# Grouping the attention exponentials by three slices and splitting three products into float16 parts

## The chip, the cores and the metric

The kernel runs on one core of one Trainium2 chip. The metric is the device time of one execution, in microseconds. The program is a chain of two attention layers with a mixture-of-experts layer between them and a "wave" layer fused behind the second attention. Five engines work side by side and meet at semaphores: TensorE (PE, with its weight loads listed apart as PEld), VectorE (DVE), ScalarE (ACT), GpSimd (POOL) and SyncE (SP, here only the issuer of DMAs).

## The reference, cut to what matters

```python
x = x + xattn0(layernorm(x), ctx, mask)      # 16 heads of 16, 2048 queries, 1601 keys
x = x + ffn(layernorm(x))                    # 2 shared and 8 routed experts, top 2
x = x + xattn1(layernorm(x), ctx, mask)
x = x + sqrt((n @ cos(theta + theta_noise))**2 + (n @ sin(phi + phi_noise))**2)   # n = layernorm(x)

def xattn(query, key, ...):
    q = query @ wq + bq;  k = key @ wk + bk;  v = key @ wv + bv
    alpha = softmax(q k^T / 4 + mask)        # per head
    return (alpha @ v) @ wo + bo

scores = sigmoid(u @ centroids)              # the router of ffn, u = layernorm(x)
```

All of it is float32. x is 2048x256, ctx is 1601x256.

## The kernel before, in words

`attention(nc, g, layer)` is called twice. Its main loop goes over 16 units (`u`): four chunks `c` of 512 queries, times four quads `q` of four heads. Inside a unit it goes over 13 key tiles `t` of 128 keys (the last has 65). So each layer has 208 tiles, the two layers 416. A tile has four slices `j`, one per head, each a bank of 128 keys x 512 queries.

What each engine does for a tile:

- TensorE, `scores(G)` (line 1260): the scores of a slice are one float32r matmul with 52 contraction rows (16 rows of the head three times, because keys and queries are held as a high and a low part, and 4 rows for shift and mask). Heads alternate between the partitions from 0 and those from 64 of `kst` and `qst` (`a` is 0 or 1, `tile_position=(HALF * a, 0)`), so two slices, one in each half of the array's rows, can run side by side. Before the change a group `G` is such a pair, and a tile has two groups (`PAIRS = 2 * KT` in a unit).
- ScalarE (line 708): one exponential for each group, 128x1024, from two PSUM banks to the float32 tile `prob`. `prob` is a ring of three tiles (`P_RING`).
- TensorE, `outputs(u, t)` (line 1274): four float32 matmuls of `v` with the four slices, side by side in four column groups of 32. Each float32 matmul is listed as two matmuls, so a tile shows x8. They gather in one of the two banks `outp`.
- VectorE, `finish(u)` (lines 903 to 914): at the end of a unit it copies the sums, takes reciprocals and scales.

The eight PSUM banks are six for scores and two for `outp`. The six are a ring of `S_RING = 3` groups of two banks. `scores(G)` waits for `exp_done >= G - S_RING + 1`, the exponential that frees its banks. The order on TensorE is written out: three groups ahead of the loop, then for each tile two `scores` (three groups ahead of the tile's own) and one `outputs`.

Between the tiles TensorE does side work at fixed tiles `t`, one piece after `outputs`: `project_out` (line 1299, quad 0 of chunks 1 to 3, t = 5, 6, 8, 9), `turn_tokens` (transposes, line 1306; quad 1 at t = 3, 4 for the next chunk's queries, quad 2 at t = 3, 5 for the finished chunk), `query` (line 1313, quad 1, t = 6, 7, 9, 10: one 128x512 float32 matmul each), in layer 0 `logits` (line 1322, quad 2, t = 8), in layer 1 `wave` (line 1330, quad 2 at t = 7, 8, 10, 11 and quad 3 at t = 4, 5, 8, 9). Side work uses the idle one of the `outp` banks. VectorE empties it: `untangle` (line 936), `split_query` (943, 945), `take_turned` (987 to 997), `take_logits` (1001), `take_wave` (1010 to 1014). In layer 0 VectorE also cuts the expert weights into float16 halves (924, 926).

Before the loop each layer projects keys (line 1142), turns the first chunk (1109), projects its queries (1149), bounds the scores, and projects values (1216). After the loop the last chunk's side work runs with nothing beside it. The sine of the wave angles is taken by ScalarE at the start of layer 1 (line 653). A branch for unsafe scores (`safe_is_off`) is not taken.

Of the kernel before, what the change touches and what calls it, by code (L numbers as in the profile page):

```python
# [4 lines left out]
F32 = mybir.dt.float32  # L5
# [8 lines left out]
P = 128  # L14
# [16 lines left out]
PARTS = 2  # L31
HALF = P // 2
# [30 lines left out]
PAIRS = 2 * KT  # L63
S_RING = 3
# [6 lines left out]
class Core:  # L71
    pass

# [23 lines left out]
def attention(nc, g, layer):  # L97
# [3 lines left out]
    with ExitStack() as es:  # L101
# [10 lines left out]
        xnT = sb("xnT", [P, DH, CH], F32)  # L112
        qparts = sb("qparts", [P, DH, PARTS, CH], F32R)
        amat = sb("amat", [P, DH, P], F32R)
        wq = sb("wq", [P, DH, D], F32)
# [18 lines left out]
        if first:  # L134
            gains = sb("gains", [P, 2, DH], F32)
            more = sb("more", [P, 2 * CH], F32)
# [9 lines left out]
        bqrow = flat_prob[0:1, KT * D + 7 * D:KT * D + 9 * D].rearrange("p (b n) -> p b n", b=2)  # L146
        slow_kst = flat_prob[:, 0:KV + 1]
# [25 lines left out]
        outp = [banks[:, 2 * S_RING + i, :] for i in range(2)]  # L173
        turn = [score[0][:, 0, :], score[0][:, 1, :]]
        pj = [score[1][:, 0, :], score[1][:, 1, :], score[2][:, 0, :]]
        nrm = score[2][:, 1, :]
        slow_score = [banks[:, 4 * i:4 * i + 4, :].rearrange("p b s -> p (b s)") for i in range(2)]
        tailbank = [score[0][:, 0, :], score[0][:, 1, :], score[1][:, 0, :], score[1][:, 1, :]]
# [25 lines left out]
        on_ready, evac_step = sem("on_ready"), sem("evac_step")  # L204
        if first:
            rows_step, rows_ready, rows_stored, xhl_stored = (
                sem(n) for n in ("rows_step", "rows_ready", "rows_stored", "xhl_stored"))
            gain_loaded, gain_ready, high_done, piece_done = (
                sem(n) for n in ("gain_loaded", "gain_ready", "high_done", "piece_done"))
# [3 lines left out]
        else:  # L213
            gathered = [sem(f"gathered{c}") for c in range(NC)]
            added, wave_done, power_ready, rooted, final_done, out_stored = (
                sem(n) for n in ("added", "wave_done", "power_ready", "rooted", "final_done", "out_stored"))
# [67 lines left out]
        def _(sp):  # L284
# [10 lines left out]
            def load_queries(u):  # L295
                b, c, quad = u % Q_RING, u // NQ, u % NQ
                if u >= Q_RING:
                    sp.wait_ge(scores_done, PAIRS * (u - Q_RING + 1))
# [67 lines left out]
            sp.dma_start(wq[:], w.wq.rearrange("(c p) n -> p c n", p=P)).then_inc(wq_loaded, 16)  # L366
# [79 lines left out]
            for u in range(UNITS):  # L446
# [17 lines left out]
                if first and u == UNITS - 1:  # L464
                    for i in range(C_RING):
                        sp.wait_ge(piece_stored[i], stored_by(i, CUTS))
                    sp.wait_ge(scores_done, PAIRS * (UNITS - 1))
# [16 lines left out]
        def _(pool):  # L484
# [104 lines left out]
            if first:  # L589
                nc.gpsimd.tensor_scalar(maskt[:], maskt[:], 4e9, -4e9, ALU.mult, ALU.add).then_inc(mask_step, 1)  # L590
            else:
                nc.gpsimd.tensor_scalar(maskt[:], masku8[:], -4e30, None, ALU.mult).then_inc(mask_step, 1)
# [52 lines left out]
        def _(act):  # L645
# [5 lines left out]
            else:  # L651
                for i in range(2):
                    nc.scalar.activation(g.wave[:, :, i, :], g.wave[:, :, i, :], ACT.Sin).then_inc(wave_done, 1)
# [8 lines left out]

            def untangle_queries():
                for h in range(DH):
                    act.wait_ge(turned, NCT + h + 1)
                    nc.scalar.activation(xnT[:, h, :], turn[h], ACT.Copy).then_inc(untangled, 1)

            def high_part(kind, o, n):
# [4 lines left out]
                else:  # L673
                    wd = CH
# [10 lines left out]
            high_part("k", 0, len(KCH) - 1)  # L685
            act.wait_ge(k_split, len(KCH))
# [15 lines left out]
            for u in range(UNITS):  # L702
                for n in range(PAIRS):
                    G, t, m = u * PAIRS + n, u * KT + n // 2, m_of(n // 2)
                    act.wait_ge(scores_done, G + 1)
                    if n % 2 == 0 and t >= P_RING:
                        act.wait_ge(pv_done, t - P_RING + 1)
# [10 lines left out]
        def _(dve):  # L718
# [100 lines left out]
            for n in range(len(KCH)):  # L819
                low_part("k", 0, n)  # L820
            if first:
                for name in queries:
                    low_part(*name)
# [1076 lines left out]
```

## Time and profile before

| what | value |
|---|---|
| median of 3 runs | 1468.65 us (1464.95 to 1470.86) |
| the profiled execution | 1466.39 us, its span 1464.6 us |
| PE busy | 1350.8 us, 92% |
| ACT busy | 1029.3 us, 70% |
| DVE busy | 683.9 us, 47% |
| granted TensorE clock, mean | 0.948 |
| main loop of layer 0 (first exponential to last one's end) | 70.35 to 477.87 us |
| main loop of layer 1 | 996.63 to 1423.55 us |

Busy shares are means over stages of different kinds. A matmul's recorded time reaches from its weights being taken to its last result, so neighbours overlap: how often starts follow each other says more than how long one lasts. Times are microseconds from the start of the span.

### The profile page before, as it was taken

What the parts mean: (1) busy time and instruction counts of PE and PEld (TensorE: products, weight loads), DVE (VectorE), ACT (ScalarE), POOL (GpSimd) and SP (SyncE); (2) the same over time, 40 slices, a digit from 0 to 9 for tenths busy, and PEclk for the clock granted to TensorE, in tenths of its full rate; (3) what the DMA queues carried; (4) which work ended last, traced back from release to release, by engine and by line L of the source; (5) the groups of instructions that cost most, each with busy time, mean ns of one, the idle gap of its engine ahead of it and who ended that gap; (6) DMA issues with size and microseconds to landing.
All of it is one profiled execution on the core that took longest, in us unless ns stands there. A gap on an engine that the chain in (4) does not pass through costs nothing. (4 is left out here: it accounts for less than half of the span.)

```text
span 1464.6 us, 23953 instructions
## 1 busy us (share of the span) xinstructions
PE 1350.8 (92%) x8958; PEld 638.7 (44%) x8959; DVE 683.9 (47%) x1281; ACT 1029.3 (70%) x1351; POOL 158.3 (11%) x184
## 2 busy tenths in 40 slices
PE   6799999999999389979999999778999999999994
PEld 3422233333323256647788888442222323323222
DVE  2454586577375537525433333441415336334245
ACT  2199989989999065423466666407898889989980
POOL 3011030020020100260000000222303001000000
PEclk8799999999999689989999999978999999999996
DMA  7766726436335160220244332576210100200001
GB/s 194 133 179 231 254 82 192 133 101 195 112 116 170 68 209 1 81 92 12 93 133 138 115 123 92 121 126 113 74 32 29 56 21 1 62 15 1 1 1 57
DMA packets 106362, 145.03 MB, mean 99 GB/s; under 512 B 23379, under 2 KB 77266, under 8 KB 106270
## 3 DMA queue, kind: packets, MB, share of 16 engines
q1 hardware_dynamic: 91264, 113.96, 26.7%
q0 software_dynamic: 6336, 19.14, 4.0%
q10 hardware_dynamic: 8670, 10.69, 3.1%
q8 instruction: 59, 0.97, 0.3%
q14 instruction: 33, 0.27, 0.1%
HBM read 78.55 MB, written 54.58 MB: 91 GB/s over the span
## 5 line engine op out<-in xcount | busy, mean ns | idle before, releaser
L708 ACT ACTIVATE prob<-banks 128x1024 f32<-128x1024 f32 (+1 forms) x832 | 770.0, 1099 | 95.5 <-PE banks L1260 91.2
L1274 PE MATMUL banks<-prob,v 128*32 128x512 f32 (+1 forms) x3328 | 448.5, 611 | 1.1 <-ACT prob L708 1.1
L1260 PE MATMUL banks<-zone,kst 52*128 52x512 f32 (+1 forms) x1664 | 343.5, 474 | 14.0 <-issue 8.8
L1260 PEld LDWEIGHTS banks<-zone,kst 52*128 52x128 f32 (+1 forms) x1664 | 140.4, 182 | 378.8 <-ACT prob L708 359.3
L1552 ACT ACTIVATE hid_d<-hp_d,b_d 128x256 f32<-128x256 f32 (+1 forms) x224 | 122.5, 547 | 150.2 <-PE hp_d L1789 71.2
L1610 DVE TENSOR_TENSOR hl_d<-hid_d,hh_d 128x256 f16<-128x256 f32 (+1 forms) x224 | 111.3, 501 | 147.7 <-ACT hh_d L1552 128.7
L1552 ACT ACTIVATE hh_d<-hp_d,b_d 128x256 f16<-128x256 f32 (+1 forms) x224 | 122.3, 546 | 0.0
L1274 PEld LDWEIGHTS banks<-prob,v 128*32 128x32 f32 (+1 forms) x3328 | 65.7, 108 | 129.1 <-issue 115.5
L908 DVE RECIPROCAL late<-late 128x512 f32<-128x512 f32 x32 | 107.3, 3353 | 1.1
L903 DVE COPY late<-banks 128x512 f32<-128x512 f32 x32 | 22.0, 688 | 109.1 <-PE banks L1274 101.9
L1789 PE MATMUL hp_d<-xsT_d,w 128*128 128x256 f16 x480 | 61.9, 281 | 2.9 <-ACT xsT_d L1568 1.5
L1789 PE MATMUL hp_d<-xsT_d,w_d 128*128 128x256 f16 x480 | 59.0, 273 | 0.0
L1800 PE MATMUL op_d<-w,hh_d 128*128 128x256 f16 x320 | 55.1, 273 | 0.0
L1800 PE MATMUL op_d<-w_d,hh_d 128*128 128x256 f16 x320 | 55.1, 273 | 0.0
L1789 PEld LDWEIGHTS hp_d<-xsT_d,w 128*128 128x128 f16 x480 | 48.2, 101 | 10.7 <-issue 3.9
L1740 PE MATMUL hp_d<-xhl_d,w_d 128*128 128x512 f16 x192 | 46.0, 400 | 7.4 <-ACT hid_d L1552 6.5
L1299 PE MATMUL banks<-wo,late 128*128 128x256 f32 x128 | 38.1, 432 | 13.5 <-DVE late L914 13.5
L1740 PE MATMUL hp_d<-xhl_d,w 128*128 128x512 f16 x192 | 43.9, 390 | 6.1 <-DMA xhl_d<-x_parts 5.7
L1789 PEld LDWEIGHTS hp_d<-xsT_d,w_d 128*128 128x128 f16 x480 | 46.6, 98 | 6.2 <-issue 0.9
L1010 DVE COPY late<-banks 128x512 f32<-128x512 f32 x16 | 11.1, 692 | 80.2 <-PE banks L1330 79.9
L1755 PE MATMUL op_d<-w_d,hh_d 128*128 128x256 f16 x256 | 44.0, 278 | 1.5 <-issue 1.5
L1541 POOL DMA_INDIRECT slot_rows<-rows_d,slot x32 | 32.6, 1017 | 112.4 <-DVE marker_d L1690 95.3
(226 smaller groups left out, 1369.2 us busy)
## 6 DMA issues: line engine op xcount, KB each, us to landing
weight_parts<-late SPq DMA_DIRECT2D x54, 256.0 KB, 2.9
zone<-q_parts SPq DMA_DIRECT2D x180, 64.0 KB
late<-in_L_ffn_W_r SPq DMA_DIRECT2D x43, 256.0 KB, 3.5
w<-weight_parts SPq DMA_DIRECT2D x5, 2048.0 KB, 9.3
w_d<-weight_parts SPq DMA_DIRECT2D x5, 2048.0 KB, 8.2
q_parts<-qparts SPq DMA_DIRECT2D x16, 512.0 KB, 5.1
weight_parts<-more SPq DMA_DIRECT2D x26, 256.0 KB, 3.3
kst<-kparts SPq DMA_DIRECT2D x64, 100.1 KB, 5.4
```

The lines of the kernel that those rows point to most:

```text
L708: nc.scalar.activation(prob[0:m, t % P_RING, 2 * (n % 2):2 * (n % 2) + 2, :], score[G % S_RING][0:m, :, :], ACT.Exp, scale=0.25).then_inc( ...
L908: nc.vector.reciprocal(spread, spread).then_inc(chain_step, 1)
L1260: last = nc.tensor.matmul(score[G % S_RING][0:m, a, :], kst[stack, 2 * q + n % 2, t * P:t * P + m].bitcast(F32R), qst[stack, u % Q_RING, n ...
L1274: last = nc.tensor.matmul(outp[u % 2][GROUP * j:GROUP * (j + 1), :], v[0:m, t, u % NQ, j, :], prob[0:m, (u * KT + t) % P_RING, j, :], star ...
L1299: last = nc.tensor.matmul(bank[:, n * D:(n + 1) * D], hpk[:, k, tokens], wo[:, k, :], start=(k == 0), stop=(k == DH - 1))
L1541: pool.indirect_dma_start(out=g.slot_dram, out_offset=bass.IndirectOffsetOnAxis(ap=g.slot[:, k, t:t + 1], axis=0), in_=rows[:, t, :, :].re ...
L1552: nc.scalar.activation(dst, hp[h % HB][:, 0:width], ACT.Gelu, bias=b1[:, b, h:h + 1], scale=1.0 / WSCALE).then_inc(gelu_done, 1)
L1610: nc.vector.tensor_tensor(hl[:, i, h, 0:width], hid[:, h % HB, 0:width], hh[:, i, h, 0:width], ALU.subtract).then_inc(hid_free, 1)
L1740: last = nc.tensor.matmul(hp[h % HB][:], w1_part(b, part, d, h), xhl[:, c, x, d, :], start=(k == 0), stop=(k == 3 * DH - 1))
L1755: last = nc.tensor.matmul(op[i][:, 0:D], a[:, n % 2, h, hs], w2_part(b, part, h), start=(h == 0 and k == 0), stop=(h == HT - 1 and k == 2))
L1789: last = nc.tensor.matmul(hp[h % HB][:, 0:T], w1_part(b, part, d, h), xsT[:, x * DH + d, :], start=(k == 0), stop=(k == 3 * DH - 1))
L1800: last = nc.tensor.matmul(op[i][:, 0:D], a[:, 0, h, i * P:(i + 1) * P], w2_part(b, part, h), start=(h == 0 and k == 0), stop=(h == HT - 1 ...
```

## The change

Two things are changed at once.

1. Slices are grouped by three: an exponential is 128x1536 from three banks, the score banks are two groups of three, and a group can span two tiles. Four groups cover three tiles. There are 278 exponentials in a layer where there were 416.
2. The query projection, the router's logits and the waves are taken with float16 operands in two parts, high and low, and three products (high x high, high x low, low x high; `PRODUCTS`), in place of one float32 matmul. Each operand is split after it is made: for the turned activations VectorE (or ScalarE before the loop) copies the high part and VectorE subtracts for the low one; the weights are scaled by 64 and split once. The logits use 16 columns and two passes. Sine is taken at the end of the experts layer, and the wave weights are split there.

```diff
+SLICES = UNITS * KT * QH
+GROUPED = 3
+GROUPS = -(-SLICES // GROUPED)
-PAIRS = 2 * KT
-S_RING = 3
+S_RING = 2
 P_RING = 3
...
+def groups_of(tiles):
+    return -(-tiles * QH // GROUPED)
...
-        banks = ps("banks", [P, 2 * S_RING + 2, CH])
-        score = [banks[:, 2 * i:2 * i + 2, :] for i in range(S_RING)]
+        banks = ps("banks", [P, GROUPED * S_RING + 2, CH])
+        score = [banks[:, GROUPED * i:GROUPED * (i + 1), :] for i in range(S_RING)]
...
+            def high_weights():
+                act.wait_ge(wq_loaded, 32)
+                nc.scalar.activation(wqp[:, 0], wq, ACT.Copy, scale=WSCALE).then_inc(wq_high, 1)
...
-            for u in range(UNITS):
-                for n in range(PAIRS):
...
-                    nc.scalar.activation(prob[0:m, t % P_RING, 2 * (n % 2):2 * (n % 2) + 2, :],
-                                         score[G % S_RING][0:m, :, :], ACT.Exp, scale=0.25).then_inc(exp_done, 1)
+            for G in range(GROUPS):
+                first_slice, n = GROUPED * G, min(GROUPED, SLICES - GROUPED * G)
+                act.wait_ge(scores_done, G + 1)
+                free = (first_slice + n - 1) // QH - P_RING + 1
+                if free > 0:
+                    act.wait_ge(pv_done, free)
+                at_slice = first_slice % (P_RING * QH)
+                nc.scalar.activation(slices[:, at_slice:at_slice + n, :], score[G % S_RING][:, 0:n, :], ACT.Exp,
+                                     scale=0.25 / WSCALE).then_inc(exp_done, 1)
...
+            def split_weights():
+                dve.wait_ge(b_loaded, 32)
+                nc.vector.tensor_scalar_mul(bqk[:, 0, :], bqk[:, 0, :], WSCALE).then_inc(bias_ready, 1)
+                dve.wait_ge(wq_high, 1)
+                nc.vector.scalar_tensor_tensor(wqp[:, 1], wq, WSCALE, wqp[:, 0], ALU.mult, ALU.subtract).then_inc(wq_split, 1)
+            def low_turned():
+                for h in range(DH):
+                    dve.wait_ge(turn_high, h + 1)
+                    nc.vector.tensor_tensor(xpT[:, 1, h, :], turn[h], xpT[:, 0, h, :], ALU.subtract).then_inc(untangled, 1)
...
+            def split_turned(bank, parts, h):
+                step[0] += 1
+                nc.vector.tensor_copy(parts[:, 0, h, :], bank).then_inc(evac_step, 1)
+                dve.wait_ge(evac_step, step[0])
+                nc.vector.tensor_tensor(parts[:, 1, h, :], bank, parts[:, 0, h, :], ALU.subtract).then_inc(side_free, 1)
...
+            def query_products(bank, o, halves_of):
+                for c in halves_of:
+                    for k, (a, b) in enumerate(PRODUCTS):
+                        last = nc.tensor.matmul(bank, wqp[:, a, c, o * P:(o + 1) * P], xpT[:, b, c, :],
+                                                start=(c == 0 and k == 0), stop=(c == DH - 1 and k == len(PRODUCTS) - 1))
+                return last
...
             def scores(G):
-                u, n = G // PAIRS, G % PAIRS
...
+                for n in range(GROUPED * G, min(GROUPED * (G + 1), SLICES)):
+                    u, t, j = n // (KT * QH), n // QH % KT, n % QH
+                    q, m, a = u % NQ, m_of(t), j % 2
...
-                pe.wait_ge(exp_done, 2 * (u * KT + t) + 2)
+                pe.wait_ge(exp_done, groups_of(u * KT + t + 1))
...
-                last = nc.tensor.matmul(side_bank("query", c, o), wq[:, k, o * P:(o + 1) * P], xnT[:, k, :], start=(k == 0), stop=(k == DH - 1))
+                last = query_products(side_bank("query", c, o), o, (k,))
...
-                    for G in (2 * (u * KT + t) + S_RING, 2 * (u * KT + t) + S_RING + 1):
-                        if G < UNITS * PAIRS:
+                    for G in range(groups_of(u * KT + t) + S_RING, groups_of(u * KT + t + 1) + S_RING):
+                        if G < GROUPS:
                             scores(G)
```

TensorE's order in the main loop, quad 0 of layer 0, three tiles, first before and then after. `zone` is where the queries lie, `kst` the keys, `prob` the exponentials; the score matmuls are L1260 before and L1315 after, those of the outputs L1274 and L1329.

```order
L1260 MATMUL banks<-zone,kst 128x512 [waits exp_done_0]
L1260 MATMUL banks<-zone,kst 128x512
L1260 MATMUL banks<-zone,kst 128x512 [waits exp_done_0]
L1260 MATMUL banks<-zone,kst 128x512
L1274 MATMUL banks<-prob,v 32x512 [waits exp_done_0]
L1274 MATMUL banks<-prob,v 32x512 x3
```

```order
L1315 MATMUL banks<-zone,kst 128x512 [waits exp_done_0]
L1315 MATMUL banks<-zone,kst 128x512 x2
L1315 MATMUL banks<-zone,kst 128x512 [waits exp_done_0]
L1315 MATMUL banks<-zone,kst 128x512 x2
L1329 MATMUL banks<-prob,v 32x512 [waits exp_done_0]
L1329 MATMUL banks<-prob,v 32x512 x3
L1315 MATMUL banks<-zone,kst 128x512 [waits exp_done_0]
L1315 MATMUL banks<-zone,kst 128x512 x2
L1329 MATMUL banks<-prob,v 32x512 [waits exp_done_0]
L1329 MATMUL banks<-prob,v 32x512 x3
```

Before, every tile reads like the first piece: two waits with two matmuls each, then the outputs. After, one tile in three has two groups of three in front of its outputs, the other two have one.

A piece of the query projection (unit 1, quad 1) on TensorE, before and after; `xnT` and `xpT` are the turned activations, `wq` and `wqp` the weights.

```order
L1313 MATMUL banks<-xnT,wq 128x512
```

```order
L1202 MATMUL banks<-xpT,wqp 128x512 [waits side_free_0,out_read_0]
L1202 MATMUL banks<-xpT,wqp 128x512 x2
```

It stands at the same place between two tiles, with three matmuls in place of one float32 matmul (which the trace lists as two).

## Rows read from the trace of the kernel before

**Rows 1.** The page: costliest groups; busy, mean ns, idle before and its releaser.
```profile
L708 ACT ACTIVATE prob<-banks 128x1024 f32<-128x1024 f32 (+1 forms) x832 | 770.0, 1099 | 95.5 <-PE banks L1260 91.2
L1260 PEld LDWEIGHTS banks<-zone,kst 52*128 52x128 f32 (+1 forms) x1664 | 140.4, 182 | 378.8 <-ACT prob L708 359.3
```
**Rows 2.** Timeline of ACT: start, length, what, count, idle before.
```profile
70.35 4.69 ACT L708 ACTIVATE prob<-banks 128x1024 f32<-128x1024 f32 x5 [31.05 <-PE banks L1260]
...
449.53 28.34 ACT L708 ACTIVATE prob<-banks 128x1024 f32<-128x1024 f32 x31 [1.25 <-PE banks L1260]
...
996.63 4.69 ACT L708 ACTIVATE prob<-banks 128x1024 f32<-128x1024 f32 x5
...
1050.03 62.05 ACT L708 ACTIVATE prob<-banks 65x1024 f32<-65x1024 f32 x68 [0.72 <-PE banks L1260]
...
1131.47 3.77 ACT L708 ACTIVATE prob<-banks 128x1024 f32<-128x1024 f32 x4 [1.87 <-PE banks L1260]
...
1420.71 2.84 ACT L708 ACTIVATE prob<-banks 128x1024 f32<-128x1024 f32 x3 [0.78 <-PE banks L1260]
```
**Rows 3.** Groups by form, ACT: busy, mean ns.
```profile
L676 ACT ACTIVATE kparts<-banks,bqk 128x512 fp32r<-128x512 f32 x12 | 8.0, 687 | 17.2 <-PE banks L1142 10.4 <-issue 6.8
...
L676 ACT ACTIVATE kparts<-banks,bqk 128x65 fp32r<-128x65 f32 x4 | 1.3, 314 | 4.8 <-PE banks L1142 4.8
```
**Rows 4.** Timeline around a query piece in layer 1, PE.
```profile
1144.86 1.06 PE L1274 MATMUL banks<-prob,v 128*32 128x512 f32 x8
1145.85 1.12 PE L1313 MATMUL banks<-xnT,wq 128*128 128x512 f32 x2
1146.91 0.73 PE L1260 MATMUL banks<-zone,kst 52*128 52x512 f32 x4
1147.57 1.06 PE L1274 MATMUL banks<-prob,v 128*32 128x512 f32 x8
```
**Rows 5.** Timeline in the score bound before the loop of layer 1: two unpaired matmuls.
```profile
969.03 0.73 PE L1164 MATMUL banks<-kparts,amat 128*128 128x512 f32 x2 [0.52 <-DVE amat L813]
```
**Rows 6.** Timeline where PE had waited: hand-over from PE to ACT and back.
```profile
1126.62 0.50 PE L1260 MATMUL banks<-zone,kst 52*128 52x512 f32 x2
1127.18 1.02 ACT L708 ACTIVATE prob<-banks 128x1024 f32<-128x1024 f32 x1 [1.18 <-PE banks L1260]
1128.26 0.49 PE L1260 MATMUL banks<-zone,kst 52*128 52x512 f32 x2 [1.13 <-issue]
```
**Rows 7.** Timeline of PE in layer 0: a piece of transposes, then the logits.
```profile
206.86 0.66 PE L1306 MATMUL banks<-ident,xn 128*128 128x128 f32 x4
207.45 0.74 PE L1260 MATMUL banks<-zone,kst 52*128 52x512 f32 x4
...
243.63 1.95 PE L1322 MATMUL banks<-cent,xnT 128*128 128x8 f32 x16
245.52 0.73 PE L1260 MATMUL banks<-zone,kst 52*128 52x512 f32 x4
```
**Rows 8.** The chain of waits: project_out, and what else stops layer 1.
```profile
1038.70 2.78 another core or an unknown queue
...
1110.89 1.06 PE banks L1299 x4
...
1127.13 1.13 issue
```
**Rows 9.** Timeline of PE in the experts: float16 matmuls of 256 columns.
```profile
539.81 0.27 PE L1755 MATMUL op_d<-w,hh_d 128*128 128x256 f16 x1
539.92 0.27 PE L1755 MATMUL op_d<-w,hl_d 128*128 128x256 f16 x1
```
**Rows 10.** Timeline outside the loops: query projection, the tail's copies and waves.
```profile
26.59 6.33 PE L1149 MATMUL banks<-xnT,wq 128*128 128x512 f32 x8 [5.56 <-ACT xnT L666]
...
959.42 5.84 PE L1149 MATMUL banks<-xnT,wq 128*128 128x512 f32 x8 [0.69 <-ACT xnT L666]
...
1445.13 1.28 DVE L987 COPY xnT<-banks 128x512 f32<-128x512 f32 x2
...
1446.56 9.74 PE L1330 MATMUL banks<-wave,xnT 128*128 128x512 f32 x16 [2.73 <-DVE xnT L987]
```
**Rows 11.** Stretches: engines' busy time, PEclk, DMA share.
```profile
959.00:963.00 4.00, 3.58 (x5) 1.50 (x6) 0.00 (x0) 0.37 (x1) 1.38 (x3) 0.50 0.30 69
```

More of the change, by code:

```diff
@@ L1144, in project_keys @@
                 last.then_inc(projected, 1)
+            def query_products(bank, o, halves_of):
[4 more added lines that the diff above has]
+                return last
             def project_queries(o):
-                bank = claim(("q", o, 0))
-                for c in range(DH):
-                    last = nc.tensor.matmul(bank, wq[:, c, o * P:(o + 1) * P], xnT[:, c, :], start=(c == 0), stop=(c == DH - 1))
-                last.then_inc(projected, 1)
+                query_products(claim(("q", o, 0)), o, range(DH)).then_inc(projected, 1)
             def bound_matrix():
+                pe.wait_ge(wq_loaded, 32)
                 pe.wait_ge(brow_ready, 1)
@@ L1231, in _ @@
                     for o in range(DH):
-                        for i in range(DH):
-                            last = nc.tensor.matmul(banks[:, DH + o, :], wq[:, i, o * P:(o + 1) * P], xnT[:, i, :],
-                                                    start=(i == 0), stop=(i == DH - 1))
-                        last.then_inc(m_query, 1)
+                        query_products(banks[:, DH + o, :], o, range(DH)).then_inc(m_query, 1)
                 pe.wait_ge(m_split, DH * (NC - 1))
@@ L1321, in logits @@
                     for h in range(DH):
-                        last = nc.tensor.matmul(bank[:, i * E_R:(i + 1) * E_R], xnT[:, h, i * P:(i + 1) * P], g.cent[:, h, :],
-                                                start=(h == 0), stop=(h == DH - 1))
+                        for a in range(PARTS):
+                            last = nc.tensor.matmul(bank[:, i * 2 * E_R:(i + 1) * 2 * E_R], xhl[:, a, h, i * P:(i + 1) * P], centp[:, h, a, :],
+                                                    start=(h == 0 and a == 0), stop=(h == DH - 1 and a == PARTS - 1))
                 last.then_inc(side_done, 1)
@@ L1329, in wave @@
                     pe.wait_ge(side_free, at["xturn", c, 1] + 1)
-                last = nc.tensor.matmul(side_bank("wave", c, i), xnT[:, h, i * P:(i + 1) * P],
-                                        g.wave[:, h, :, :].rearrange("p a n -> p (a n)"), start=(h == 0), stop=(h == DH - 1))
+                for k, (a, b) in enumerate(PRODUCTS):
+                    last = nc.tensor.matmul(side_bank("wave", c, i), xpT[:, b, h, i * P:(i + 1) * P], g.wave[:, a, h, :],
+                                            start=(h == 0 and k == 0), stop=(h == DH - 1 and k == len(PRODUCTS) - 1))
                 if h == DH - 1:
@@ L1559, in _ @@
                 if n == 0:
[L1560 removed]
+                    nc.scalar.activation(g.gate[:], g.gate[:], ACT.Exp, scale=-1.0 / WSCALE).then_inc(exp_done, 1)
             def load_rows(step):
@@ L1871, in program @@
             attention(nc, g, 0)
-        g.wave = sb("wave", [P, DH, 2, D], F32)
+        g.wave = sb("wave", [P, PARTS, DH, 2 * D], F16)
         experts(nc, g)
```

141 lines of the change are left out of this document (79 added, 62 removed).

## The prediction

> **What bounds the kernel now.** I read the page first, then ACT's timeline, then PE's timeline in the loops, then groups by form. The page shows two loops that make 834 of 1464.6 us, and in them each of two engines waiting for the other: ACT's exponentials were kept idle 95.5 us, nearly all by the score matmuls, and the score matmuls' weight loads 379 us by the exponentials [rows 1]. The reader is to find out who sets the pace, and when. Between side work it is ACT: 68 exponentials follow each other in 62.05 us, the last lasting 1.02, so one takes (62.05 - 1.02)/67 = 0.911 us and a tile 1.822 [rows 2, 6]. PE, when nothing keeps it, starts a tile's outputs 0.66 after its scores and goes on 0.99 later: 1.65 a tile [rows 4]. So PE has 0.17 us of slack in a tile, and side pieces that cost it 0.59 to 1.89 each eat that slack and then stop ACT. The floor of ACT is 416 x 0.911 = 379.0 us a layer; layer 0's loop took 477.87 - 70.35 = 407.5, layer 1's 1423.55 - 996.63 = 426.9 [rows 2].
>
> **The exponentials, on ACT.** The slope of an ACT instruction is (687 - 314)/(512 - 65) = 0.834 ns a column [rows 3]; 0.911 us is then 0.854 of columns and 0.057 of fixed cost. The change leaves the columns and removes 2 x (416 - 278) = 276 fixed costs: 276 x 0.057 = 15.7 us. An exponential of 1536 takes 1.338 us, 1.784 a tile. Its result comes 1.02 + 0.43 = 1.45 after its start.
>
> The Trainium skill ("ScalarE: Activation LUTs", What ACT_TABLE_LOAD costs) gives 186 ns plus 0.833 ns a column and an overlap of 93 ns back to back. The slope agrees with the trace; its fixed part of 93 ns doesn't, and by it the saving would be 25.7 us. The trace decides here.
>
> **The scores, on PE.** This is the part that I think decides. Four slices as two pairs last 0.73 from first start to last end [rows 4]. Two unpaired float32r matmuls of 512 columns last 0.73 too [rows 5], one or one pair alone 0.50 [rows 6]. So a slot costs 0.23 whether one matmul or two are in it. A group of three is a pair and a lone one: two slots, as much as a whole tile's four slices before. Before, three tiles had six slots; now they have eight, unless the lone matmul of a group finds the next group's first beside it. That needs the next group's wait to be over when the lone one starts.
>
> It isn't, because the ring has two groups now. I call groups S, their exponentials E, the outputs of a tile V, and start the clock where S5, the group of a tile with one, starts. S5 ends at 0.73, and E5 starts 0.06 later (the hand-over is 1127.18 - 1127.12 [rows 6]), at 0.79, and is done at 2.24. PE does V from 0.66 and S6 from 1.65, whose lone matmul starts at about 2.0. S7 needs the banks of E5: 2.24 and 0.05 for the way back [rows 6] is 2.29. The pairing is missed by 0.3 us and PE is idle for about as long. S7 then takes its own 0.66, V 0.99 (to 3.94), S8 and V 1.65 (to 5.59), and there the next round starts. ACT needs 4 x 1.338 = 5.35 in the round and is behind PE by a few hundredths at one of the waits, so I take 5.63 us for three tiles: 1.877 a tile against 1.822. Bounds: 5.35 if pairing is had after all (ACT then sets it), 5.75 if every switch between groups costs 0.04 more. For 208 tiles 5.63 is 390.3 us, 11.3 over the old floor in each layer.
>
> **The side work.** Before, a float32 piece took 1.06 us (1146.91 - 1145.85), transposes 0.59, logits 1.89, project_out 1.06 [rows 4, 7, 8]. Layer 0 has 12 + 12 + 12 + 3 pieces: 12.7 + 7.1 + 12.7 + 5.7 = 38.2 us; layer 1 has 24 waves in the loop in place of the logits: 57.9 us. A float16 matmul of 256 columns starts 0.11 after the one before [rows 9], so three of 512 take 0.65, and with the 0.20 that the float32 piece has beyond its two 0.43 passes, 0.85: 0.21 less a piece, 12 pieces in layer 0 and 36 in layer 1. Logits keep 16 passes with a cheaper weight load; estimate 1.6. New sums: 34.8 and 50.4.
>
> What matters is how much is absorbed. Before, layer 0 lost 28.5 us over the floor; I count 3 of it as the loop's start, so 12.7 of 38.2 was absorbed in PE's slack. Layer 1 lost 47.9, of which 2.8 and about 3 are waits for something outside the loop (the gathers of chunk 1 and the sums behind them) [rows 2, 8], so 16 of 57.9 was absorbed. After the change PE has no slack but the 0.3 us in front of S7, and only a piece that falls ahead of it, one in three, can use it: 39/3 x 0.3 = 4 us in layer 0, 6 in layer 1.
> Layer 0: 390.3 + 34.8 - 4 + 3 = 424.1, against 407.5: +16.6.
> Layer 1: 390.3 + 50.4 - 6 + 5.8 = 440.5, against 426.9: +13.6; the gathers have more time in a slower loop, but I leave that. Together +30.2.
>
> **The rest.** Before each loop the query projection goes from 8 float32 passes (6.33 and 5.84 us, mostly at the lower clock of 0.50) to 12 float16 ones: at that clock 12 x 0.43 = 5.2, at full clock 2.6 [rows 10, 11]. Against it VectorE splits the weights (about 0.75, with its bias step 0.9) in a chain where it has no gap, and subtracts the low parts of the turned queries (0.7 more until PE may start): +1.6 - (0.6 to 3.7), so -2 to +1 a layer; I take 0. If ACT's copy of the weights (0.5) holds back the key loads, it adds that. At the end of layer 1 VectorE has two subtractions more (1.28 became two of 0.64, four make 2.6): +1.3, and the waves, 6 passes of 0.43 each at the low clock against 4 of 0.43 x 2, 2.6 against 3.4 for the first: -0.8 and then VectorE's three steps a wave set the pace as before: +0.5 to +1.5, take +1. Layer 0's tail loses a float32 copy: -0.7. The sine and its split lie beside the last results' way to HBM and cost nothing; uncovered they cost 4. In the loop VectorE's extra 0.7 a turned half comes two tiles ahead of the query piece that needs it. Sum of the rest: about +1, bounds -4 and +7.
>
> **The sum.** The profiled execution is 1466.39 us: 1466.4 + 30.2 + 1 = 1497.6. The median of the runs is 2.3 above it: 1500. I put it 1 higher, since an emptied ring of two is refilled with fewer exponentials in hand than one of three: 1501 us.
>
> **Rivals.**
> A. The lone matmul is not lost, and ACT stays the bound: 5.35 us a round. Speaks for it: adjacent groups alternate halves (0, 1, 0 then 1, 0, 1), and ACT does get shorter by 15.7 us. Against it: the step above, S7's wait ends 0.3 us too late. It would give -15.7 and the 3.4 + 7.5 of side work less: 1469 - 26.6 + 1 = 1443.
> The Trainium skill ("TensorEngine Tiling (Array Packing)", Key Properties) says that tiles of the array operate independently and can load weights and multiply in parallel; by it the lone matmul could share its slot, and the kernel would come out as in A. The trace shows pairs that do so [rows 4], always of one group; none across a wait.
> B. Pairing is had about where side work delays PE, and the round is near 5.45: the loops' gain in ACT and in side work (27) is paid back by absorbing half as much (14 less) and 0.1 a round (14). It ends at 1469, no change.
> C. My forecast: PE sets the pace, 1501.
> D. PE sets the pace and in addition the ring of two makes every side piece stop ACT fully and makes the next exponential late too: 99 pieces at 0.3 more, 1531. For it: after a piece S waits and E are in series, 0.73 + 0.06 + 1.45 + 0.05. Against it: an exponential of 1.34 covers most of a piece of 0.85.
>
> **How the numbers follow.** A 0.08, B 0.08, C 0.74, D 0.10. About 0.5%, 7 us, is what a measurement of this kernel can tell from no change. Faster by more: A, 0.09 with the edge of B. Same: 0.09, B and a little of C. Slower: 0.82. The range takes C with the round's 5.5 and 5.75 (-18 and +17 over 139 rounds), the rest's -4 and +7 and half of D: 1479 to 1521.
>
> **What would show it.** Right: ACT's rows of 128x1536 start 1.33 to 1.34 apart only where two follow without a gap; idle ahead of the exponentials caused by the score matmuls grows from 91 us to above 120, though ACT's busy time falls; PE's three tiles between side pieces take 5.6 us, with an idle of about 0.3 ahead of the second group of the tile that has two; the float16 piece takes 0.85; the loops take about 424 and 440 us. Wrong: if unhindered tiles go at 1.78 with ACT gapless (A), if a group of three lasts less than 0.7 on PE from start to end, or if ACT's gaps after side pieces are over a microsecond (D). If the loops are as said and the time isn't, the error is in the stages before or behind them.

## The result and the profile after

The changed kernel took 1514.18 us (median of 4 runs, 1508.92 to 1520.6) against 1468.59 us for the kernel before (4 runs). The ratio is 1.0318, with a 95% interval of 1.0284 to 1.0351: 3.2% slower. The forecast was 1501 us, with a range of 1479 to 1521; the time is 13 us above the one and inside the other. The profiled execution took 1515.61 us with a span of 1513.4 us, against 1466.39 and 1464.6 before.

The page's costliest groups, after (columns as in [rows 1]):

```profile
L731 ACT ACTIVATE prob<-banks 128x1536 f32<-128x1536 f32 x556 | 769.4, 1450 | 149.5 <-PE banks L1315 141.4
L1315 PE MATMUL banks<-zone,kst 52*128 52x512 f32 (+1 forms) x1664 | 386.4, 463 | 39.9 <-DVE centp L1082 23.3
L1315 PEld LDWEIGHTS banks<-zone,kst 52*128 52x128 f32 (+1 forms) x1664 | 159.1, 184 | 386.6 <-ACT prob L731 300.6
```

They answer to [rows 1]. The exponentials are fewer by a third, but ACT's busy time stands (770.0 to 769.4), because this sum counts each from its start to its last result. Their idle time rose from 95.5 to 149.5 us, and nearly all of it (141.4) is a wait for the score matmuls. The prediction wanted above 120 there, but some 19 of the 141.4 are the late start below: with that mended (the first experiment) the wait is 114.1. The second row has what was not expected: PE's scores waited 23.3 us for VectorE's `centp`.

ACT's timeline cuts the span in five stages. The starts and ends are those of the first and last exponential of each loop.

| stage, us | before | after | difference | predicted |
|---|---|---|---|---|
| start to the first exponential | 70.35 | 88.16 | +17.8 | 0 |
| loop of layer 0 | 407.5 | 422.3 | +14.7 | +16.6 |
| between the loops | 518.8 | 515.2 | -3.5 | 0 |
| loop of layer 1 | 426.9 | 446.1 | +19.2 | +13.6 |
| last exponential to the end | 41.1 | 41.6 | +0.6 | +1 |

The loops are where the prediction had them. The start is not.

**The start.** The timeline of all engines between 60 and 89 us, after:

```profile
64.21 10.26 SPq L364 DMA_DIRECT2D zone<-q_parts  x18
75.58 7.52 SPq L291 DMA_DIRECT2D kst<-kparts  x12
85.69 0.17 DVE L1074 TENSOR_SCALAR gains<-gains 128x4 f32<-128x4 f32 x1 [21.64 <-DMA kst<-kparts]
86.34 0.18 DVE L1082 SCALAR_TENSOR_TENSOR centp<-cent,centp 128x16 f16<-128x16 f32 x1
86.87 1.65 PE L1315 MATMUL banks<-zone,kst 52*128 52x512 f32 x6 [23.34 <-DVE centp L1082]
```

and ACT's own timeline:

```profile
88.16 5.55 ACT L731 ACTIVATE prob<-banks 128x1536 f32<-128x1536 f32 x4 [50.46 <-PE banks L1315]
```

VectorE stands idle for 21.64 us, until the loads of all four quads' keys are in (its program waits for each), then does the small operations on the gains and the split of the centroids, and only then may PE start its first scores. PE needs the keys of one quad for them. The split itself takes under a microsecond; it stands behind a wait for data that it doesn't use. ACT's first exponential had waited 31.05 us before [rows 2], and waits 50.46 now.

**The round.** ACT's timeline in the loop of layer 1, away from side work:

```profile
1095.98 11.08 ACT L731 ACTIVATE prob<-banks 128x1536 f32<-128x1536 f32 x8 [0.19 <-PE banks L1315]
1107.25 11.06 ACT L731 ACTIVATE prob<-banks 128x1536 f32<-128x1536 f32 x8 [0.19 <-PE banks L1315]
```

Eight exponentials are two rounds of three tiles. Two rounds take 1107.25 - 1095.98 = 11.27 us, one 5.63: the predicted figure. ACT is busy nearly throughout and still doesn't set the pace: four exponentials would need 4 x 1.338 = 5.35, but each stretch ends with 0.2 us of waiting for the scores, and inside one they follow each other at (11.08 - 1.45)/7 = 1.376.

PE's timeline in layer 0, with a query piece at its head:

```profile
142.30 1.07 PE L1329 MATMUL banks<-prob,v 128*32 128x512 f32 x8
143.30 0.82 PE L1202 MATMUL banks<-xpT,wqp 128*128 128x512 f16 x3
144.05 0.91 PE L1315 MATMUL banks<-zone,kst 52*65 52x512 f32 x6
144.89 1.06 PE L1329 MATMUL banks<-prob,v 128*32 128x512 f32 x8
146.27 0.73 PE L1315 MATMUL banks<-zone,kst 52*128 52x512 f32 x3 [0.31 <-ACT prob L731]
146.93 1.06 PE L1329 MATMUL banks<-prob,v 65*32 65x512 f32 x8
147.93 0.73 PE L1315 MATMUL banks<-zone,kst 52*128 52x512 f32 x3
148.59 1.06 PE L1329 MATMUL banks<-prob,v 128*32 128x512 f32 x8
149.58 1.44 PE L1315 MATMUL banks<-zone,kst 52*128 52x512 f32 x6
150.96 1.07 PE L1329 MATMUL banks<-prob,v 128*32 128x512 f32 x8
```

A group of three has the outputs behind it start 0.66 later (147.93 to 148.59): as long as four slices took [rows 4]. A tile with two groups takes 149.58 to 150.96 = 1.38 when nothing has held PE up, and 144.05 to 144.89 = 0.84 behind a query piece. In the second case ACT had had time to free the banks, so the wait of the second group was over, and the two lone matmuls shared a slot. (One of its groups belongs to the short tile of 65 keys; the 12 others of this kind in layer 0 take about 0.89.) But most of what this saves is lost at once: the next group starts 146.27 - 144.89 = 1.38 after the outputs in place of 0.99, 0.31 of it a wait for the exponential that frees its banks. The query piece occupies PE for 144.05 - 143.30 = 0.75 us, against 0.85 predicted and 1.06 before [rows 4].

The logits of a chunk, PE's timeline in layer 0:

```profile
270.40 0.56 PE L1378 MATMUL banks<-centp,late 128*128 128x16 f16 x16
270.89 0.96 PE L1315 MATMUL banks<-zone,kst 52*128 52x512 f32 x6
```

They occupy 0.49 us, where 1.6 was estimated and 1.89 measured before [rows 7].

### The profile page after: what moved, and what is told of

Read it like the earlier page. It is cut to its first block and busy times, and to the rows that moved or that the text cites. A ratio compares the mean times of both kernels' runs of the same rounds, so it can differ in the third digit from the quotient of the medians.

```text
span 1513.4 us, 23968 instructions
## 1 busy us (share of the span) xinstructions
PE 1371.2 (91%) x9022; PEld 644.3 (43%) x9023; DVE 702.7 (46%) x1315; ACT 1029.5 (68%) x1076; POOL 158.1 (10%) x184
## 5 line engine op out<-in xcount | busy, mean ns | idle before, releaser
L731 ACT ACTIVATE prob<-banks 128x1536 f32<-128x1536 f32 x556 | 769.4, 1450 | 149.5 <-PE banks L1315 141.4
L1329 PE MATMUL banks<-prob,v 128*32 128x512 f32 (+1 forms) x3328 | 451.2, 615 | 0.1
L1315 PE MATMUL banks<-zone,kst 52*128 52x512 f32 (+1 forms) x1664 | 386.4, 463 | 39.9 <-DVE centp L1082 23.3
L1315 PEld LDWEIGHTS banks<-zone,kst 52*128 52x128 f32 (+1 forms) x1664 | 159.1, 184 | 386.6 <-ACT prob L731 300.6
L1329 PEld LDWEIGHTS banks<-prob,v 128*32 128x32 f32 (+1 forms) x3328 | 65.9, 108 | 157.5 <-issue 138.9
L1803 PE MATMUL hp_d<-xhl_d,w_d 128*128 128x512 f16 x192 | 42.7, 379 | 3.6 <-ACT hid_d L1608 2.8
```

Of the source, the lines that this page charges most:

```text
L731: nc.scalar.activation(slices[:, at_slice:at_slice + n, :], score[G % S_RING][:, 0:n, :], ACT.Exp, scale=0.25 / WSCALE).then_inc(exp_done, 1)
L1315: last = nc.tensor.matmul(score[G % S_RING][0:m, n % GROUPED, :], kst[stack, 2 * q + j // 2, t * P:t * P + m].bitcast(F32R), qst[stack, u ...
L1329: last = nc.tensor.matmul(outp[u % 2][GROUP * j:GROUP * (j + 1), :], v[0:m, t, u % NQ, j, :], prob[0:m, (u * KT + t) % P_RING, j, :], star ...
L1803: last = nc.tensor.matmul(hp[h % HB][:], w1_part(b, part, d, h), xhl[:, c, x, d, :], start=(k == 0), stop=(k == 3 * DH - 1))
```

## The experiments

All are written as edits of the changed kernel or of the one before. For each the four numbers in brackets are: the start of the first exponential, the loop of layer 0, what lies between the loops, and the loop of layer 1, in us. The chips differ: the kernel before took 1442 us on one and 1461 to 1469 on others, and the traces from that one are some 14 us shorter between the loops. The kernel before wasn't traced there. So ratios are taken on one chip; that chip ran the first four experiments.

### The split of the centroids ahead of the keys

Of the changed kernel, in VectorE's program; the copies and the subtraction that make `centp` move with the block that is shown:

```
+if first:
+    dve.wait_ge(g.cent_loaded, 16)
+    nc.vector.memset(centp[:], 0.0).then_inc(cent_step, 1)
...
 for quad in range(NQ):
     dve.wait_ge(k_loaded[quad], 16 * QH * len(K_STACK))
...
     dve.wait_ge(gain_ready, 1)
-    dve.wait_ge(g.cent_loaded, 16)
-    nc.vector.memset(centp[:], 0.0).then_inc(cent_step, 1)
...
```

> The changed kernel with the four VectorE instructions that split the centroids put ahead of VectorE's waits for the keys of all four quads. Theory (TensorE's first scores of layer 0 were kept 17.8 us by a small split that stood in VectorE's order behind the last key load): the first exponential starts near 70 us in place of 88, the time falls by 15 to 18 us, to about 1498. Rival (the late start hid loads that TensorE would have waited for anyway): under 5 us, with new waits for q_parts or kst in the first unit.

Measured: 1468.65 us against 1441.99 for the kernel before beside it, ratio 1.0176 (1.0144 to 1.0207); [68.06, 420.8, 504.8, 437.1]. Timeline, all engines:

```profile
65.36 0.17 DVE L1073 TENSOR_SCALAR centp<-cent 128x16 f16<-128x16 f32 x1
65.56 0.17 DVE L1075 SCALAR_TENSOR_TENSOR centp<-cent,centp 128x16 f16<-128x16 f32 x1
67.00 0.69 PEld L1316 LDWEIGHTS banks<-zone,kst 52*128 52x128 f32 x6 [4.08 <-issue]
67.03 1.38 PE L1316 MATMUL banks<-zone,kst 52*128 52x512 f32 x6 [3.66 <-issue]
68.06 4.21 ACT L731 ACTIVATE prob<-banks 128x1536 f32<-128x1536 f32 x3 [30.54 <-PE banks L1316]
```

The first exponential is back at 68, 20 us earlier, and the wait of ACT ahead of it at 30.5, as before. No new wait for loads takes its place, so the rival falls. The ratio falls from 1.0318 to 1.0176, by 1.4%, and 20 us are 1.4% of this time. The two ratios come from different chips. So some 1.4 of the 3.2% is the place of four operations of under 0.2 us each, and 1.8% remain.

### Pairs with float16 products

Of the kernel of the last experiment:

```
-GROUPED = 3
+GROUPED = 2
...
-S_RING = 2
+S_RING = 3
```

> As the last, and slices grouped by two again with a ring of three groups: the float16 products alone. Theory (grouping by three costs TensorE two more slots in three tiles, the float16 products save 0.31 us a piece): layer 0's loop about 404, layer 1's about 420 us, the time 1450 to 1456. Rival (VectorE's extra subtractions pay back what TensorE saves): 1464 to 1472.

Measured on the same chip: 1430.23 us, ratio 0.992 (0.9894 to 0.9946); [68.74, 401.2, 505.0, 410.2]. The page's group of the exponentials, and the last stretch of ACT's timeline in layer 0:

```profile
L731 ACT ACTIVATE prob<-banks 128x1024 f32<-128x1024 f32 x832 | 772.2, 1185 | 70.1 <-PE banks L1316 69.0
```

```profile
395.36 74.56 ACT L731 ACTIVATE prob<-banks 128x1024 f32<-128x1024 f32 x81 [0.79 <-PE banks L1316]
```

This is faster than both kernels, by 0.8% than the one before. Layer 1's loop is 10 us shorter than the expectation's 420; the ratio would be 1457 us on the chip of the result, just past the expected 1450 to 1456. The idle time ahead of the exponentials is 70.1 us in place of 95.5 before and 119.4 with groups of three (the last experiment's page). The two kernels differ in the grouping alone (and with it in the ring, two groups of three banks or three of two): threes cost 420.8 - 401.2 = 19.6 us in layer 0 and 437.1 - 410.2 = 26.9 in layer 1.

### Groups of three with the float32 products

Of the kernel before, with the loops over groups on ACT and PE as the change has them:

```
-PAIRS = 2 * KT
-S_RING = 3
+GROUPED = 3
+S_RING = 2
```

> The kernel before with the grouping by three alone, float32 products as before. Theory (TensorE sets the pace, side pieces of 1.06 us added nearly in full): layer 0's loop 428 to 432, layer 1's 448 to 455, the time 1510 to 1520; unhindered rounds of three tiles 5.63 us. Rival (the grouping is neutral and the float16 operands and their splits cost the time): 1462 to 1475.

Measured on the same chip: 1492.56 us, ratio 1.0349 (1.0319 to 1.0379); [69.27, 432.4, 501.5, 446.2]. Timelines of ACT, then of PE:

```profile
1071.22 11.07 ACT L718 ACTIVATE prob<-banks 128x1536 f32<-128x1536 f32 x8 [0.20 <-PE banks L1270]
1082.48 11.06 ACT L718 ACTIVATE prob<-banks 128x1536 f32<-128x1536 f32 x8 [0.19 <-PE banks L1270]
```

```profile
1087.30 1.45 PE L1270 MATMUL banks<-zone,kst 52*128 52x512 f32 x6
1088.68 1.06 PE L1284 MATMUL banks<-prob,v 128*32 128x512 f32 x8
```

The round is 1082.48 - 1071.22 = 11.26 for two, and the two-group tile 1.38 again: the round does not depend on the products. The grouping alone costs 3.5%, more than the whole change with the centroids mended (1.8%). Layer 1's loop came out just under the expected 448 to 455, layer 0's at the top of its 428 to 432. Float16 products therefore give 1492.56 - 1468.65 = 24 us beside threes, but 1441.99 - 1430.23 = 12 us beside pairs. That with pairs part of a piece lay in PE's slack, and with threes nearly every piece is on the path, would explain it; no trace of the kernel before on this chip shows it.

### A narrow lone matmul

The third matmul of each group does 64 of its 512 columns in layer 1; the rest of its slice is left out.

```
+wide = 64 if n % GROUPED == 2 and G >= 2 * S_RING and not first else CH
-last = nc.tensor.matmul(score[G % S_RING][0:m, n % GROUPED, :],
+last = nc.tensor.matmul(score[G % S_RING][0:m, n % GROUPED, 0:wide],
...
-                        qst[stack, u % Q_RING, j // 2, :].bitcast(F32R),
+                        qst[stack, u % Q_RING, j // 2, 0:wide].bitcast(F32R),
```

> The first kernel of this call with the third matmul of every group cut to 64 of 512 columns in layer 1 (the rest of those scores is left out). It takes the lone slot's cost and leaves waits, ring and exponentials. Theory (the lone matmul's slot makes TensorE the bound): unhindered rounds of three tiles fall from 5.63 to ACT's 5.35 us, exponentials 1.34 apart without gaps, layer 1's loop falls by 15 to 20 us. Rival (the ring of two and its hand-overs set 5.63, whatever the lone matmul costs): rounds stay within 0.05 of 5.63.

Measured, one run: 1439.65 us; [68.77, 419.8, 501.4, 406.1]. Timelines of ACT, then of PE, layer 1:

```profile
1041.19 61.90 ACT L731 ACTIVATE prob<-banks 128x1536 f32<-128x1536 f32 x46 [0.70 <-PE banks L1317]
```

```profile
1044.15 0.53 PE L1317 MATMUL banks<-zone,kst 52*128 52x512 f32 x3
1044.62 1.07 PE L1331 MATMUL banks<-prob,v 128*32 128x512 f32 x8
1046.73 0.52 PE L1317 MATMUL banks<-zone,kst 52*128 52x512 f32 x3 [0.59 <-ACT prob L731]
```

A group now occupies 1044.62 - 1044.15 = 0.47 us, 0.19 less, and layer 1's loop is 31 us shorter than beside it (406.1 for 437.1), while layer 0's, which was left alone, stands (419.8 for 420.8). ACT runs without a gap: (61.90 - 1.45)/45 = 1.343 us an exponential, 5.37 a round. So the slot of the lone matmul is what makes PE the bound, and ACT has 1.343 for the predicted 1.338. The loop fell by more than the expected 15 to 20: the rounds give 69 x (5.63 - 5.37) = 18 us, and the rest fits side work that now falls into PE's slack, since PE would need only 4 x 0.47 + 3 x 0.99 = 4.85 us a round (an estimate from the rows above). With pairs the same loop took 410.2: even with the slot nearly gone, threes gain only 4 us there, about as much as this loop moves between two traces of one kernel.

### Short exponentials

The exponentials of layer 1 go over two of a group's three slices; the third is left out. PE's work is as it was.

```
+ if not first and n == GROUPED and G >= 2 * S_RING * P_RING:
+     n = 2
```

> The first kernel of the earlier call (centroids split early, groups of three) with each exponential of layer 1 over two of its group's three slices (the third is left out). It takes 0.43 us off the exponential and leaves TensorE's work as it is. Theory (the lone matmul fails to pair because the next group's wait, on the exponential just running, ends 0.3 us too late): the wait is now over in time, the six matmuls of the tile with two groups take three slots and start its outputs after 0.84 to 0.90 us, not 1.3 to 1.4, and a round of three tiles takes 5.05 to 5.15 us. Rival (a lone matmul never shares its slot with the next group): six matmuls keep 1.3 us and the round stays at 5.6.

Measured, one run, on a chip where the kernel before took 1462.59: 1469.62 us; [69.07, 422.2, 517.2, 417.1]. Timelines of ACT, then of PE, layer 1:

```profile
1077.93 2.92 ACT L733 ACTIVATE prob<-banks 128x1024 f32<-128x1024 f32 x3 [0.63 <-PE banks L1318]
1081.48 1.02 ACT L733 ACTIVATE prob<-banks 128x1024 f32<-128x1024 f32 x1 [0.63 <-PE banks L1318]
1083.14 2.91 ACT L733 ACTIVATE prob<-banks 128x1024 f32<-128x1024 f32 x3 [0.63 <-PE banks L1318]
```

```profile
1082.37 0.96 PE L1318 MATMUL banks<-zone,kst 52*128 52x512 f32 x6
1083.26 1.06 PE L1332 MATMUL banks<-prob,v 128*32 128x512 f32 x8
```

The round is 1083.14 - 1077.93 = 5.21 us instead of 5.63 (5.05 to 5.15 were expected), though no matmul was removed: the six matmuls of a two-group tile now take 1083.26 - 1082.37 = 0.89 instead of 1.38. The loop takes 417.1, where the changed kernel took 442.3 on this chip (the next section). With the banks free in time PE does put the lone matmuls side by side. This is the mechanism of rival A, and what kept it away in the changed kernel is the time of the exponential in a ring of two, the prediction's step.

### The two kernels again

Without an edit: the kernel before, and the changed kernel, on the chip of the last experiment.

> The kernel before, unchanged, for its loops on this chip. Nothing to tell apart: layer 0's loop about 404 to 408 us; if the gathers of layer 1 wait less here than in the first trace, layer 1's loop is 417 to 422 in place of 427.

> The changed kernel, unchanged, for its loops on the same chip. If the 1.5 us for which TensorE waited for a turned tile in the second unit of layer 1 is VectorE being late by its new subtraction, it comes again, with the clock at 0.5 behind it; if it was the gathers' time on the first chip, the wait is under 0.3 us and layer 1's loop near 437.

Measured: 1461.27 us, [68.17, 407.3, 516.0, 426.9], and 1513.19 us, [88.20, 420.2, 518.7, 442.3]. The loops of the kernel before came out as in its first trace to 0.2 us; the shorter loop of 417 to 422 that the expectation held possible didn't come. Of the changed kernel neither case came: PE doesn't wait for the split of the turned half, and the loop is still 5 us over 437. The changed kernel's first loop is 2.1 us and its second 3.8 us shorter than in its first trace, and between the loops 2.7 us over the kernel before instead of 3.5 under. Stage by stage these two traces differ by 20.0, 12.9, 2.7, 15.4 and 0.9 us. So the stages between the loops carry no gain, and layer 1's loop holds something that moves between executions.

One thing that moves is a pause of ACT early in layer 1. ACT's timeline of the kernel before, this run:

```profile
1037.07 5.61 ACT L708 ACTIVATE prob<-banks 128x1024 f32<-128x1024 f32 x6 [2.73 <-remote]
```

ACT idles 2.73 us, released by nothing of its own core (the first trace has it too: the "unknown queue" of the chain [rows 8]). In the changed kernel's first trace, ACT and PE at that place, and the stretch behind it (columns as in [rows 11]):

```profile
1065.82 1.45 ACT L731 ACTIVATE prob<-banks 128x1536 f32<-128x1536 f32 x1 [2.68 <-DMA weight_parts<-late]
```

```profile
1063.41 1.06 PE L1329 MATMUL banks<-prob,v 128*32 128x512 f32 x8
1066.00 0.63 PE L1361 MATMUL banks<-ident,xn 128*128 128x128 f32 x4 [1.52 <-DVE xpT L979]
1066.56 1.75 PE L1315 MATMUL banks<-zone,kst 52*128 52x512 f32 x6
```

```profile
1066.00:1074.00 8.00, 7.96 (x32) 2.16 (x32) 1.38 (x2) 5.52 (x4) 0.00 (x0) 0.60 0.06 16
```

The view names a DMA that ACT does not wait for; the pause is as long as before. VectorE stood too (3.73 us until 1064.44, by the view "remote"), so its split of the turned half came late, and PE stood for 1.52 us. Its granted clock was 0.60 in the eight microseconds behind, which is mostly the lower of its two levels, 1.2 GHz. In the second trace ACT has no such pause: its longest idle time there is 1.64 us, for the scores, PE stood for 1.10 us with no releaser in the view, the clock stayed at 1.00, and the loop was 3.8 us shorter.

There is a second place of this kind, some 100 us further on, where layer 1's sixth unit begins. PE in the kernel before (its first trace), and the stretch behind (columns of the second line as in [rows 11]):

```profile
1132.55 0.80 PE L1260 MATMUL banks<-zone,kst 52*128 52x512 f32 x2 [2.36 <-ACT prob L708]
1132.00:1139.00 7.00, 6.45 (x30) 1.64 (x34) 4.94 (x6) 5.61 (x7) 0.00 (x0) 0.58 0.02 4
```

and in the changed kernel:

```profile
1168.98 0.73 PE L1315 MATMUL banks<-zone,kst 52*128 52x512 f32 x3 [1.98 <-ACT prob L731]
1173.00:1181.00 8.00, 8.00 (x34) 2.60 (x32) 1.90 (x3) 3.10 (x3) 0.00 (x0) 0.55 0.00 0
```

PE's clock falls behind it in both kernels. VectorE idles at this place too, 6.5 to 7.2 us ahead of its copy of the finished sums, in all traces but the four of the chip that ran the first four experiments; there it is 2.4 to 3.1 us, PE and ACT show no stop, and the first pause is missing as well. So the 437.1 us of the first experiment is layer 1's loop without the stops, and the 442.3 and 446.1 of the changed kernel hold them. What stops the engines is open.

### The float16 products as the change wrote them

Of the changed kernel, the centroids' split left where it is:

```
-GROUPED = 3
+GROUPED = 2
...
-S_RING = 2
+S_RING = 3
```

> The changed kernel with GROUPED = 2 and S_RING = 3 and the centroids' split left where the change has it: the float16 products alone, as the change wrote them. Theory (the wait for the centroids' split and the grouping are separate terms that add up): the first exponential of layer 0 starts near 88 as in the changed kernel, the loops take 400 to 403 and 409 to 413 us as with the pairs and the early split, and the ratio to the kernel before is 0.992 + 0.014 = 1.006, between 1.002 and 1.009. Rival (the late start costs only in the ring of two, because the ring of three has more scores in flight when they may start): first exponential at 88, but the time no more than 5 us over the pairs with the early split, ratio under 0.998.

Measured: 1466.54 us against 1467.8 for the kernel before beside it, ratio 0.9991 (0.9954 to 1.0029); [87.21, 399.1, 523.6, 418.0]. The waits of PE name the same split for a start as late as in the changed kernel (us in total, times, longest):

```profile
PE banks L1315 <- DVE centp L1082: 23.9, 1, 23.9
```

The start is as expected, the ratio lies between the two theories: 0.7% (about 0.3 to 1.2%) over the pairs with the early split, where 1.4% were expected from the threes. Layer 1's loop took 418.0, over the expected 409 to 413: this trace has the stop at the sixth unit (PE stood for 1.22 and 1.23 us), which the pairs with the early split didn't have on their chip. The runs were on different chips, and those of this kernel spread over 1456 to 1478 us. Whether some of the late start is given back later with a ring of three, or whether the two chips differ, stays open. What is shown: as the change wrote them, the float16 products alone bring nothing that can be measured.

### The second half turned later

```
-if t in (3, 4):
-    turn_tokens("turn", c + 1, t - 3, xn)
+if t in (3, 5):
+    turn_tokens("turn", c + 1, (t - 3) // 2, xn)
```

> The changed kernel with the second half of the turned activations (and of the turned expert outputs) turned one tile later, after tile 5 in place of tile 4, so that VectorE's split of the first half has a tile more. Theory (in layer 1 TensorE's transposes wait up to 1.5 us for VectorE's split, and the stall and the lower clock behind it make the loop 2 to 5 us longer than it would be): no wait of the transposes for the split in the loop, layer 1's loop 437 to 441 us, ratio to the changed kernel's 1.0318 lower by 0.002 to 0.003. Rival (the stall of one execution moves about and costs nothing on the mean; the loop is long because TensorE sets its pace): loop 441 to 446, ratio within 0.002 of the changed kernel's.

The kernel that ran had the centroids' split in its early place too, which the expectation doesn't say; so it is held against the first experiment (1.0176, loop 437.1) and not against the changed kernel. That one ran on the chip without the stops, so only the wait and the pause can be compared, not the whole loop. Measured: 1499.82 us, ratio 1.0207 (1.0154 to 1.0261); [67.27, 422.2, 523.2, 449.3]. ACT, PE and the stretch behind, layer 1:

```profile
1054.02 4.21 ACT L731 ACTIVATE prob<-banks 128x1536 f32<-128x1536 f32 x3 [2.90 <-DMA weight_parts<-late]
```

```profile
1051.57 0.73 PE L1316 MATMUL banks<-zone,kst 52*128 52x512 f32 x3
1055.52 1.22 PE L1316 MATMUL banks<-zone,kst 52*128 52x512 f32 x3 [3.22 <-ACT prob L731]
1056.67 1.93 PE L1330 MATMUL banks<-prob,v 128*32 128x512 f32 x8
```

```profile
1055.00:1065.00 10.00, 9.48 (x32) 2.89 (x32) 1.84 (x3) 4.68 (x4) 0.00 (x0) 0.50 0.00 0
```

No transposes wait for VectorE's split any more, and the loop is no shorter: the longest of all. The theory's 437 to 441 us didn't come. Whether the rival is right this run can't say, since its terms were set against the changed kernel's ratio. The pause of ACT is there, 2.90 us; PE has used up its two groups of banks, stands for 3.22 us, and then does a group in 1.22 us and a tile's outputs in 1.93, at a granted clock of 0.50, the lower level, for ten microseconds. In the kernel before, PE lost 0.56 us to the pause of 2.76 and its clock stayed at 1.00; it had a query piece to do meanwhile, besides a ring of three. So these traces show side by side that a pause as long costs the changed kernel more, and that the low clock comes with it. That the ring of two is the reason is argued and not shown.

## Why the prediction was right in the loops and wrong at the start

**The round of three tiles: right.** 5.63 us predicted, 5.63 measured, with float16 and with float32 products. The two experiments on layer 1 take the two halves of the reason apart: a shorter lone matmul makes ACT the bound (5.37), and an earlier exponential lets the lone ones share a slot (5.21). In the changed kernel neither happens.

**Side work: right in sum.** A query piece took 0.75 for 0.85 (12 of them: 1.2 us less) and the logits 0.49 for 1.6 (three: 3.3 less). A piece ahead of the two-group tile gets back 1.38 - 0.89 = 0.49 where 0.3 was allowed, but behind eight of the 13 such tiles of layer 0 the next group waits and 1.38 - 0.99 = 0.39 is lost again: 13 x 0.49 - 8 x 0.39 = 3.2 us for the 4 of the sum. Together 424.1 - 1.2 - 3.3 + 0.8 = 420.4, and the loop took 420.2 and 422.3 in the changed kernel's two traces, 420.8 with the early split. The 2.1 us between the changed kernel's two traces lie in the loop's start: the first six exponentials took 101.30 - 88.16 = 13.1 us in the one and 11.0 in the other, where the pace of the round is 8.4 and the sum allowed 3 more. Gaps of ACT over a microsecond, which the prediction had as the sign of D, are there behind the second of two project_out pieces (1.26 and 1.27 us in the first experiment's trace, the pieces being 1.06 us each); they did not add up to D.

**Layer 1: 440.5 predicted, 437.1 to 446.1 measured in three traces** (the early split once, the changed kernel twice). The forecast lies inside, in part by luck. It holds 5.8 us for waits from outside, taken over from before as they were; the 437.1 comes from the chip whose traces show no stops in the loop, and without them the sum is 434.7 (it has no term for the loop's start, for which layer 0's has 3). The other two lie 5 and 9 us higher, with the stops and the clock of 0.50 to 0.60 behind them.

**Between and behind the loops: right.** Nothing measurable between on one chip (518.7 against 516.0); 0.6 at the end for 1 predicted.

**The start: the step that failed.** The prediction priced the removed and added work ahead of the loops at about 0 and counted the VectorE operations that it names there by their length. The centroids' split isn't among them, and it did not look at what PE's new wait on it is queued behind: VectorE's wait for the keys of all four quads. That is 17.8 of the 48.8 us, and no term of the sum held it; mended, the ratio is 1.0176. The other four stages measure 14.7 - 3.5 + 19.2 + 0.6 = 31.0 us where the sum had 30.2 + 1. That this agrees to 0.2 us is luck: the stages miss by -1.9, -3.5, +5.6 and -0.4. And the time lies inside the range because the round, the rest and half of D had been given room that they didn't use; the room wasn't for this. With the missing term the profiled execution would have been forecast at 1466.4 + 31.2 + 17.8 = 1515.4; it took 1515.6. The 4.5 us between 1518.7, which that makes for the median (1515.4 + 2.3 + 1), and the measured 1514.2 are the step from a profiled execution to the median: 2.3 + 1 was added, and here the median is 1.4 below.

**The rivals.** A's mechanism exists and was missing by a few tenths of a microsecond, as argued; the time was far from its 1443. By the rule of the Trainium skill ("TensorEngine Tiling (Array Packing)", Key Properties), that tiles operate independently, the lone matmul could share its slot: the short exponentials show that it does across two groups (0.89 us for six), and the changed kernel shows that it doesn't when a wait stands between them (1.38). B needed pairing about half of the time and a loop as before; C held.

## What to carry to other kernels

Where matmuls share a slot in pairs, a group of odd size leaves a lone one that takes a whole slot: count slots, not instructions, on the engine with the least slack. Ask of a larger instruction what ring it leaves: two groups of three hold as many banks as three of two, but the wait for a free group ends later. And read each new wait from the side of the engine that signals it: not how long the signalled work is, but what stands ahead of it in that engine's order.

## What the runs showed of the hardware

- Two row-tiled matmuls of 512 columns share a slot of 0.23 us only where no unfinished wait stands between them: six in 0.84 to 0.90 us or in 1.38, by the same instructions.
- Sixteen float16 matmuls of 16 columns take 0.49 us to the next, where the float32 ones of 8 columns took 1.89.
- A stop of PE of 1.52 us in a busy loop was followed by a granted clock of 0.60 over eight microseconds, one of 3.22 us by 0.50 over ten, stops of 1.98 and 0.78 us close together by 0.55 over eight; after one of 1.10 us it stayed at 1.00. In the kernel before it was 0.58 over seven behind stops of 1.13 and 2.36 us.
- At one place of layer 1 VectorE idled 6.5 to 7.2 us, with stops of ACT and PE beside it, in seven traces, and 2.4 to 3.1 us without them in the four of one chip. What it is is open.
- An exponential over 1536 columns costs 1.343 us back to back (the run with the narrow lone matmul), within 0.005 of what the slope of [rows 3] and the fixed 0.057 gave.
